# A decoder layer on one core: attention by chunks of 128 tokens with running states

## What is computed

```
ig, fg = [q,k,v] @ gate weights + biases;  cs = cumsum(log_sigmoid(fg))
log_D[s,t] = cs[s] - cs[t] + ig[t] for t <= s, else -inf;  m[s] = max_t log_D[s,t]
C = (q k^T / 8) * exp(log_D - m);  norm = max(|sum_t C|, exp(-m))
h = (C / (norm + 1e-6)) v;  LN(h) * ln_scale
```

## Time and profile before

| | us |
|---|---|
| three runs | 2101.17, 2101.32, 2106.62 (median 2101.32) |
| span of the profiled execution | 2102.4 |
| PE busy | 1752.4 |
| DVE busy | 910.9 |
| ACT busy | 511.5 |
| POOL busy | 293.3 |

### The profile page before, as it was taken

One profiled execution on the slowest core, in us unless ns is written; L12 is line 12 of the kernel. 1 busy time (PEld: TensorE's weight loads), 2 busy tenths in 40 slices (PEclk: granted clock), 3 DMA queues, 4 the chain that ended last, 5 costly groups with the idle time before them and its releaser, 6 DMA issues.

```text
span 2102.4 us, 30288 instructions
## 1 busy us (share of the span) xinstructions
PE 1752.4 (83%) x11084; PEld 1530.2 (73%) x11122; DVE 910.9 (43%) x2170; ACT 511.5 (24%) x1237; POOL 293.3 (14%) x365
## 2 busy tenths in 40 slices
PE   3488988889898976423799999999999999999980
PEld 1266666566666664223799999999999999999980
DVE  5538879687888776568211111111111111111117
ACT  1444445354544442100111111111111111111110
POOL 2001110102010111100021221211211211212202
PEclk9798989899899988655999999999999999999995
DMA  5303140404132110330267667667676677676609
GB/s 150 80 1 81 41 121 1 122 1 121 56 86 41 41 41 1 158 152 0 97 211 281 231 224 264 228 238 252 225 256 245 214 272 243 211 280 232 222 10 325
DMA packets 89967, 318.27 MB, mean 151 GB/s; under 512 B 42582, under 2 KB 42588, under 8 KB 79516
## 3 DMA queue, kind: packets, MB, share of 16 engines
q1 hardware_dynamic: 80156, 296.26, 38.6%
q0 software_dynamic: 9728, 20.98, 6.1%
HBM read 280.91 MB, written 36.31 MB: 151 GB/s over the span
## 4 chain that ended last, share of the span: by engine, by line
PE 71%; DVE 18%; issue 6%; ACT 3%; POOL 1%; DMA 1%; DVEq 0%; POOLq 0%; ACTq 0%; another core or an unknown queue 0%
PE bank L761 30%; PE bank L774 15%; PE bank L534 5%; PE bank L605 5%; PE bank L589 5%; DVE arena L1025 2%; DVE arena L1328 2%; PE bank L740 1%; PE bank L562 1%; DVE arena L1019 1%; PE bank L536 1%; PE bank L556 1%; PE bank L653 1%; DVE arena L1054 1%; PE bank L741 1%
## 5 line engine op out<-in xcount | busy, mean ns | idle before, releaser
L761 PE MATMUL bank<-arena 128*128 128x160 f32 x4608 | 638.7, 300 | 0.6 <-issue 0.6
L761 PEld LDWEIGHTS bank<-arena 128*128 128x128 f32 x4608 | 630.9, 191 | 1.1 <-issue 0.7
L1440 DVE TENSOR_TENSOR arena<-arena,bank 128x160 f32<-128x160 f32 x256 | 82.3, 322 | 828.8 <-ACT arena L978 823.3
L774 PE MATMUL bank<-arena 128*128 128x160 f32 x2304 | 321.5, 300 | 1.0 <-DVE arena L1442 1.0
L774 PEld LDWEIGHTS bank<-arena 128*128 128x128 f32 x2304 | 313.8, 190 | 2.4 <-issue 1.2
L589 PE MATMUL bank<-arena 128*128 128x128 f32 (+2 forms) x896 | 182.9, 348 | 57.5 <-DVE arena L1054 54.5
L978 ACT ACTIVATE arena<-bank 128x160 f32<-128x160 f32 x288 | 87.6, 304 | 563.0 <-PE bank L761 561.2
L1575 POOL DMA_INDIRECT acc_rows<-arena,keep x64 | 95.6, 1493 | 830.2 <-DVE arena L1429 793.9
L589 PEld LDWEIGHTS bank<-arena 128*128 128x128 f32 x896 | 136.8, 209 | 84.0 <-DVE arena L1054 68.7
L605 PEld LDWEIGHTS bank<-arena 128*128 128x128 f32 x1280 | 172.6, 212 | 16.5 <-issue 1.8
L605 PE MATMUL bank<-arena 128*128 128x96 f32 x1280 | 170.7, 295 | 2.3 <-issue 2.0
(11 more groups left out here) (199 smaller groups left out, 1653.9 us busy)
## 6 DMA issues: line engine op xcount, KB each, us to landing
arena<-in_wup SPq DMA_DIRECT2D x32, 4096.0 KB, 12.1
arena<-in_wdn SPq DMA_DIRECT2D x32, 2048.0 KB, 7.8
arena<-in_aup SPq DMA_DIRECT2D x32, 512.0 KB, 11.3
arena<-in_xT SPq DMA_DIRECT2D x8, 1024.0 KB, 5.4
arena<-in_kT SPq DMA_DIRECT2D x8, 1024.0 KB, 7.9
arena<-in_kT SPq DMA_DIRECT2D x16, 512.0 KB, 8.8
arena<-in_v SPq DMA_DIRECT2D x32, 256.0 KB, 9.3
x_rows<-arena SPq DMA_DIRECT2D x8, 1024.0 KB, 4.5
```

The lines of the kernel that those rows point to most:

```text
L761: m = pe.matmul(u[:, g * CAP:(g + 1) * CAP], w, xeT[:, c, :], start=(c == 0), stop=(c == C - 1))
L774: m = pe.matmul(Db[k][:, c * CAP:(c + 1) * CAP], w, hact[:, j, :], start=(j == 0), stop=(j == J))
L1440: dve.tensor_tensor(hact[:, j, :], sg[k], u, ALU.mult).then_inc(up_v(f"mul{j}"), 1)
```

## The change

Attention is computed chunk by chunk. Only the four diagonal 128 x 128 blocks of a head are formed as scores; earlier chunks reach a chunk through a state (64 x 65 per head) that sums k v^T with decay weights, one for each of the first three chunks. Two heads are done at a time: head r of a pair uses partitions r*64 to r*64+63 for scores and state products, in two PSUM banks side by side. What belongs to it:

- `scores(b, j)`: 8 matmuls of 64 rows and 128 columns for a pair. `kz` is gone, `kT` is double buffered.
- `broadcast_max`: a second matmul adds -1e30 above the diagonal; POOL's `mask` is gone, and `decays` is four Exps.
- New: `broadcast_decay` (PE, 384 columns for a pair) and `scale_queries` (DVE); `weigh_values` (POOL); `state` (PE, 24 matmuls and 4 tiny ones); `first_state` (ACT); `later_states` (DVE); `gate_chunks` (POOL) and `gates_f` (ACT) for the exponents.
- `weigh` is one operation of 1024 columns for a pair, `head_out` handles a pair.
- `norm1_out` and `norm3_out` move to ACT; POOL computes the shift for them (`affine`). The router's variance and length come from sums that ACT forms (`accum_out` of norm 3 and `squares`); DVE's second bn_stats is gone.
- Absolute value and Relu of the forget gate move from DVE to ACT.
- `step` is written anew on all engines.

```diff
-            def scores(b, h, chunks):
...
-                        m = pe.matmul(Sb[k % 2][:, at:at + n], kz[b.slot][:, h % 2, h // 2, tb * P:(tb + 1) * P],
-                                      qT[b.slot][:, h // 2, q * P:q * P + n], start=True, stop=True)
+            def scores(b, j):
...
+                for tb in range(TB):
+                    rows = slice(tb * P, (tb + 1) * P)
+                    for r in range(2):
+                        half = slice(r * DH, (r + 1) * DH)
+                        m = pe.matmul(Sp[:, r * T + tb * P:r * T + (tb + 1) * P], kT[b.slot][half, j, rows],
+                                      qT[b.slot][half, j, rows], start=True, stop=True)
...
+                pe.matmul(Bb[:, :], identh, upper_h.rearrange("p a t -> p (a t)"), start=True, stop=False)
+                pe.matmul(Bb[:, :], sel[:, h, :], bfs[b.slot], start=False, stop=True).then_inc(bc_t(f"bc{h}"), 1)
...
+            def broadcast_decay(b, j):
...
+                pe.matmul(Bb[:, 0:INT], selF[0:NH, j, :], Fr[b.slot][0:NH, :], start=True, stop=True)\
+                    .then_inc(fb_t(f"f{j}"), 1)
...
+            def state(b):
+                pe.wait_ge(*ga_a.at("w", b))
...
+                pe.wait_ge(*st_p.at("vw", b))
+                for q in range(TB - 1):
...
+                    for h in range(NH):
+                        half = slice(h % 2 * DH, h % 2 * DH + DH)
+                        m = pe.matmul(dst[half, h // 2 * VW:(h // 2 + 1) * VW], va[b.slot][:, q, h * VW:h * VW + DH],
+                                      vw[:, q, h, :], start=True, stop=True)
...
+            def values(b, j):
...
+                for r in range(2):
+                    h = 2 * j + r
+                    for tb in range(TB):
+                        pe.matmul(Pp[:, r * T + tb * PVN:r * T + (tb + 1) * PVN],
+                                  Dm[j % 2][:, r * T + tb * P:r * T + (tb + 1) * P],
+                                  va[b.slot][:, tb, h * VW:h * VW + PVN], start=(tb == 0), stop=False)
+                pe.wait_ge(*qs_v.at(f"qs{j}", b))
...
+                for q in range(TB - 1):
+                    for r in range(2):
+                        half = slice(r * DH, (r + 1) * DH)
+                        at = r * T + (q + 1) * PVN
+                        m = pe.matmul(Pp[:, at:at + VW], qs[j % 2][half, q * P:(q + 1) * P], St[half, q, j, :],
+                                      start=False, stop=(q == TB - 2))
...
+            def scale_queries(b, j):
+                dve.wait_ge(*fb_t.at(f"f{j}", b))
...
+                dve.tensor_tensor(qs[j % 2], qT[b.slot][:, j, P:T], Bb[:, 0:INT], ALU.mult).then_inc(qs_v(f"qs{j}"), 1)
...
+            def norm1_out(b):
+                act.wait_ge(*n1_p.at("shift", b))
+                for tb in range(TB):
+                    act.activation(x1[b.slot][:, tb, :], x1[b.slot][:, tb, :], ACT.Identity, scale=rs1[:, tb:tb + 1],
+                                   bias=nb1[:, tb:tb + 1]).then_inc(n1_a(f"out{tb}"), 1)
...
+            def weigh_values(b):
...
+                pool.tensor_tensor(vw, src, wcol[:, 0:TB - 1].unsqueeze(3).to_broadcast([P, TB - 1, NH, VW]), ALU.mult)\
+                    .then_inc(st_p("vw"), 1)
```

More of the change, by code:

```diff
@@ new lines, in decoder_kernel @@
+        qs_v = steps("qscale_vector", [f"qs{j}" for j in range(NP)])
+        st_p = steps("state_pool", ["vw"])
+        st_t = steps("state_tensor", ["r"] + [f"p{q}" for q in range(TB - 1)])
+        st_a = steps("state_scalar", ["S0"])
+        st_v = steps("state_vector", ["m1", "S1", "m2", "S2"])
+        ev_v = steps("ev_vector", [x for j in range(NP) for x in (f"neg{j}", f"den{j}", f"eps{j}", f"rec{j}", f"out{j}")])
+        l2_v = steps("ln2_vector", ["bn2", "aggr2", "scaled", "sum", "bn3", "aggr3"])
@@ L427, in load_context @@
             def load_context(b):
[L428 to L433, removed]
+                sp.wait_ge(*pv_t.at(f"pv{NP - 1}", b - 2))
+                sp.dma_start(kT[b.slot], kT_d[b.line(1)]).then_inc(ld_k[b.slot], 16)
                 for tb in range(TB):
@@ new lines, in step @@
+                if s:
+                    broadcast_max(n - 1, 4)
+                if a:
+                    gates_k(n)
+                if r:
+                    router_in(n - 2, a)
+                if s:
+                    broadcast_max(n - 1, 5)
+                if a:
+                    queries(n)
+                if s:
+                    broadcast_decay(n - 1, 1)
+                    values(n - 1, 1)
+                    scores(n - 1, 2)
+                if s:
+                    broadcast_max(n - 1, 6)
@@ new lines, in step @@
+                if a:
+                    gates_q(n)
+                if r:
+                    router_hidden(n - 2, 0, a)
+                    router_hidden(n - 2, 1, a)
+                if s:
+                    broadcast_max(n - 1, 7)
+                    broadcast_decay(n - 1, 2)
+                    values(n - 1, 2)
+                    scores(n - 1, 3)
+                if r:
+                    router_stats(n - 2, a)
+                    router_hidden_stats(n - 2)
+                if s:
+                    broadcast_decay(n - 1, 3)
@@ new lines, in step @@
+                if s:
+                    decays(n - 1, 5)
+                if x1:
+                    inputs(n + 1, 0)
+                if a:
+                    queries(n)
+                if r:
+                    squares(n - 2)
+                if s:
+                    decays(n - 1, 6)
+                if a:
+                    gates_1(n)
+                if s:
+                    decays(n - 1, 7)
+                if x1:
+                    inputs(n + 1, 1)
+                    inputs(n + 1, 2)
```

742 lines of the change are left out of this document (390 added, 352 removed).

## The result

The changed kernel takes 2117.3 us (median of 4 runs, 2114.1 to 2119.8), the kernel before 2101.2 in the same session: a ratio of 1.0067, 95% interval 1.0055 to 1.0079. It is slower by 0.7%, where 2060 us (range 2003 to 2096) had been forecast. The profiled execution has a span of 2118.0 us for 2102.4. Of all runs behind this text one, of 2769.6 us at a mean granted clock of 0.626 (the second kernel of experiment 8), was in a slower state and is left out.

A forecast was written before the change was run, and what follows sets the result against it. No engine is full: TensorE and VectorE take turns in the pipelined steps, with a low clock in thin stretches. From 2102.4, -2 - 3 - 16 - 18 - 2 + 1 = -40 and -1.1 give 2061.3, rounded 2060 us, range 2003 to 2096.

The forecast's parts named there:

- the walk: Timeline through a full step, wait by wait: some 17 us idle, 92.4 us for 95.2, -18 over six steps.
- PE runs retention and broadcasts to 18.2: Head of a full step: TensorE does retention and row broadcasts from t = 0 to 18.2 us, no wait named.
- over 99: Sign that the forecast is wrong: a full step takes over 99 us, where 90 to 95 was expected.
- two thin stretches: Times in a full step with little TensorE work, lowering the clock: 32 to 38 and 59 to 72 us.
- Between both halves running together and a drain ... I take 0: 64-row matmuls on TensorE: halves overlapping (-6 us) against drains at changes of shape (+4), taken as 0 a step.
- the query copies: ScalarE's copies of queries after norm 1's output, with two PSUM tiles: TensorE idle 1.0 and 3.8 us.
- the statistics' wait: ScalarE's copy of router statistics stands behind gates 3, 4 and f: TensorE idle 3.8 us, to 71.6.
- the port charge of 2 us: VectorE slowed beside GpSimd's long multiply by a shared SBUF port: 2 us a full step, bounds 0 and 4.
- step 1: Pipeline step without router: forecast to end at 71 to 76 us for 91.4, a gain of 16.
- (A): Rival, work counts, not waits: engines slip past waits and halves overlap, full step 82, total 2000 us; chance 0.20.
- (B): Rival, router's detour: late statistics copy starves TensorE and lowers the clock, full step 100.4, total 2111 us; chance 0.10.
- (C): Rival, nothing arrives: full steps at 99 us, total 2101 us, the idle sum unchanged; chance 0.08.

The follow-up runs named there:

- experiment 8: Changed kernel with thrown-away TensorE matmuls before retention 1's rows in each step with a router: 14 gave 2147.2 us, 7 (second kernel) gave 2115.1 us.
- experiment 1: Changed kernel with ScalarE's raw rows of norm 1 in a buffer of their own: 2079.6 us, 0.9891 of before.
- experiment 2: Changed kernel with VectorE's norms 2 and 3 moved to the end of the step before, same buffer: 2080.1 us, 0.989 of before.
- experiment 6: Changed kernel with own raw-row buffer, statistics copy first, taps and decays 5 sooner, `retained(2)` a place earlier: 2048.8 us, 0.9745 of before.
- experiments 9: Kernel of experiment 6 with two thrown-away matmuls in TensorE's wait for norm 1's first output: 2027.1 us, 0.9656 of before.
- experiment 10: Kernel of experiments 9 with one more thrown-away matmul ahead of the decay row of head pair 2: 2005.1 us, 0.9537 of before.
- experiment 11: Changed kernel with score matmuls issued head by head, not alternating between the array's halves: 2149.0 us, 1.0215 of before.
- experiment 3: Changed kernel with ScalarE's copy of the router statistics ahead of gates 3, 4 and f: 2114.9 us, 1.0059 of before.
- experiment 4: Changed kernel with both the own raw-row buffer and the statistics copy ahead of gates 3, 4 and f: 2067.4 us, 0.9833 of before.

## Why the prediction was wrong

**The step that failed** is in the walk: "PE runs retention and broadcasts to 18.2". PE got there at 27.7 (505.63 less 477.9), 6.5 us idle and 2.8 us at the low clock later: a wait of PE that the walk put at nothing without a reason. It followed DVE's norm 2 (it starts at 6.6, where the text says 7) and PE's banks each by itself, and never asked what the raw rows overwrite. Its own numbers had the answer: 7 and 5.6 for norm 2 and 2.7 for `sum` make 15.3 (15.1 in the trace), where PE is ready for retention 2 at 9.7. In the kernel before the same wait stood in the code and cost nothing, because retention 2 came after the values of two heads; the change moved it ahead of them. Taken away, it gives 37.7 of the 57.3 us between forecast and result (experiment 1), and shortened by another way it gives as much (experiment 2). The sign "over 99" for a full step came true, with 102.6 us.

**The clock** probably carries much of the rest; no run takes it out of the changed kernel by itself. The walk had two thin stretches, the trace has three beside the front one (values at 3.73, 3.63 and 3.66 us in step 5 for 2.02 at the high clock). With the front wait gone steps 2 to 6 have 94.7 us in the mean for 92.4 forecast, at 13.8 us of idle time for the 17 walked (the idle times that the walk names add up to 15.8): less waiting, slower work. In step 5 of the kernel before the clock fell once. In the kernel of experiment 6 two thin stretches filled gave 44 us (experiments 9 and 10), more than the whole forecast gain.

**TensorE's work.** "Between both halves running together and a drain ... I take 0" was on the wrong side of the middle: sixteen score records take 1.04 us from start to start (509.15 to 510.19), 0.065 each for the 0.11 taken; twelve from the states 0.72, 0.06 each for 0.11; the states 0.034 for 0.07, below their own bounds of 0.06 to 0.12. Over a step that is 2.9 + 2.4 + 1.7 = 7 us less at full clock, so that about 14 of PE's work were gone, and the busy time still reads 83.6. The Trainium skill (TensorEngine Tiling (Array Packing), Theoretical Speedup) states up to 2x for a contraction of up to 64; the 1.66 us by head and 1.11 in turns of experiment 11 are 1.5x. Of the drain at a change of shape, taken at 0.25 us each without a row, the trace shows nothing: values end at 508.49, and the products with the states start at 508.43.

**What held.** DVE at 62 us for 60; idle 10.4 us ahead of `retained(1)`, released by ACT's inputs, for 11.5; the query copies at 1.03 and 3.50 for 1.0 and 3.8; the statistics' wait of 5.09 for 3.8; `scale_queries(2)` at 0.87 and head 7 at 1.23 were less than the 3.1 and 2.7 walked; before head 7 ACT's table load ran while it waited for PE and was hidden. One weighting takes 1.22 us for the 1.21 worked out from the earlier trace rows. POOL's multiply takes 2.80 us for 3.4, at a moment when DVE idles, so the port charge of 2 us, taken from the earlier trace rows, was not paid here. Steps 8 and 9 are within 1 us, the experts the same, start and step 0 at -3.6 for -5. What didn't hold: step 1 at 81.0 for 71 to 76 (clock 0.73), and the low clock four times in step 5, where two were forecast.

**Rivals.** (A), waits slip and 2000 us: neared only by experiment 10, by other means. (B): its 2111 us is near, and its full steps of 100.4 are 100.6 in the mean (603.3 by six), but by another wait; its own, for the statistics copy, gives nothing when taken away (experiment 3), and 12 us once the front wait is gone (experiment 4). Its size was met by luck. (C): no. The range ended at 2096 because every bound was drawn around waits that I had found; none covered one that I had not.

## What to carry to other kernels

When an order is rewritten, list for each moved instruction all its waits, the ones for a buffer's last reader too, and ask where each producer now stands; a wait that cost nothing may only have been covered by its place. Where two of TensorE's banks alternate, a late copy stops everything behind it. And price a gap on TensorE twice, as waiting and as clock: here cheap thrown-away matmuls in two waits took 2.1% off the kernel of experiment 6. They must fit into the wait (experiment 8).

## What the runs showed that was not expected

- Thrown-away work makes this kernel faster: 2.9 us of matmuls in a step of about 88 us, nearly all of it inside waits, gave 22 us for the first two and 22 for the third, in medians of four runs that spread over 14 to 18 us.
- The granted clock differs from run to run of one kernel: 2106.6 to 2116.3 us with 0.874 to 0.867, 2021.2 to 2038.8 us with 0.888 to 0.876.
- Before retention 2, a gap of 2.1 to 2.5 us left it at 3.67 to 3.70 us (experiment 2), one of 6.1 to 6.5 brought it to 5.8 to 6.4 (the changed kernel).
- Matmuls of 64 rows on the two halves overlap only when they alternate: sixteen records in 1.11 us in turn, in 1.66 by head.
- ACT's `accum_out` costs a record of 0.19 us beside the 0.80 of the output itself.
